# Decoder layer with routed experts: base rows gathered in the slot that uses them, two transpose groups placed side by side, and another order at the start of self-attention

## The reference

```python
x = x + attn(layernorm(x))               # attn(r) = r + p @ v, q = layernorm(r): 4 heads of 128,
                                         # 2048 fixed keys and values, p = relu(q @ k.T)**2
x = x + xattn(layernorm(x), ctx, mask)   # 16 heads of 64 over 128 context rows, softmax
x = x + ffn(layernorm(x))
# ffn: a shared SwiGLU (512 -> 1024 -> 512) and routed experts, top 1 of 32
e = argmax(x @ gate_w);  xs = x * sigmoid(max(x @ gate_w))
routed = (silu(xs @ Wg[e]) * (xs @ Wu[e])) @ Wd[e]     # Wg, Wu: 32 x 512 x 1024, Wd: 32 x 1024 x 512
out = shared(x) + routed
```

## Time and profile before

| | us |
|---|---|
| median of 3 runs (2825.84 to 2826.16) | 2826.04 |
| profiled execution | 2824.46 |
| its span, first to last instruction | 2822.8 |
| PE busy in it | 2761.5 (98%) |
| DVE busy | 1783.8 (63%) |
| POOL busy | 1063.0 (38%) |

### The profile page before, as it was taken

How to read it: one execution, slowest core, us unless ns; L and a number is a source line. 1 busy time by engine, 2 the same in 40 slices (tenths; PEclk the granted TensorE clock), 3 DMA queues, 4 the chain that set the end, 5 groups by cost and what they waited for, 6 DMA issues and landing times.

```text
span 2822.8 us, 46193 instructions
## 1 busy us (share of the span) xinstructions
PE 2761.5 (98%) x13287; PEld 2279.2 (81%) x13289; DVE 1783.8 (63%) x2600; ACT 1592.6 (56%) x2748; POOL 1063.0 (38%) x692
## 2 busy tenths in 40 slices
PE   7999999999999999999999999999999999999998
PEld 6888888888878888788778888887788888888886
DVE  6556565666876665667653333346795765677776
ACT  7888888888765554566621111112675644465665
POOL 6888888887622221122200000000342422333333
PEclk9999999999999999999999999999999999999999
DMA  1000000002231102110321111113896865787884
GB/s 64 27 27 11 26 26 26 11 30 63 83 98 46 45 30 90 39 37 27 112 93 63 60 59 59 59 59 111 323 355 211 326 217 166 257 299 239 294 288 174
DMA packets 191367, 326.90 MB, mean 116 GB/s; under 512 B 23592, under 2 KB 49192, under 8 KB 190784
## 3 DMA queue, kind: packets, MB, share of 16 engines
q1 hardware_dynamic: 180016, 300.81, 31.1%
q0 software_dynamic: 11280, 25.20, 2.6%
HBM read 288.95 MB, written 48.76 MB: 120 GB/s over the span
## 4 chain that ended last, share of the span: by engine, by line
PE 79%; issue 9%; DVE 5%; ACT 2%; POOL 2%; DMA 1%; ACTq 0%; DVEq 0%; POOLq 0%; SPq 0%
PE d_pG L1993 8%; PE d_pU L1993 8%; PE a_pS L47 4%; PE a_pS L49 4%; PE a_pS L48 4%; PE a_pO L47 4%; PE a_pO L49 4%; PE a_pO L48 4%; PE d_pD L49 3%; PE d_pD L47 3%; PE d_pD L48 3%; PE c_pD L49 2%; PE c_pD L47 2%; PE c_pG L47 2%; PE c_pD L48 2%
## 5 line engine op out<-in xcount | busy, mean ns | idle before, releaser
L158 POOL TENSOR_TENSOR a_pL<-a_p,a_pH 128x1024 fp32r<-128x1024 f32 x256 | 618.3, 2418 | 152.3 <-DVE a_p L345 149.9
L345 DVE TENSOR_TENSOR a_p<-a_r,a_pS 128x1024 f32<-128x1024 f32 x256 | 312.2, 1220 | 259.4 <-ACT a_r L166 254.2
L1229 DVE TENSOR_TENSOR e_wL<-e_raw,e_wH 128x1024 fp32r<-128x1024 f32 x384 | 450.1, 1217 | 33.8 <-PE d_pU L1993 23.1
L1224 ACT CAST e_wH<-e_raw 128x1024 fp32r<-128x1024 f32 x384 | 384.5, 1054 | 85.6 <-PE d_pD L49 59.5
L683 POOL TENSOR_TENSOR b_S<-b_S,b_ri 128x512 f32<-128x512 f32 x128 | 133.2, 1041 | 478.5 <-DVE b_ri L844 478.5
L166 ACT ACTIVATE a_r<-a_pS 128x1024 f32<-128x1024 f32 x256 | 261.8, 1023 | 78.8 <-PE a_pS L49 76.7
L166 ACT ACTIVATE a_pH<-a_r 128x1024 fp32r<-128x1024 f32 x256 | 271.9, 1062 | 9.1
L1473 POOL DMA_INDIRECT out<-d_og,c_iw x46 | 124.0, 2695 | 340.5 <-DVE d_og L1867 340.5
L700 ACT ACTIVATE b_S<-b_S,b_nm 128x128 f32<-128x128 f32 x512 | 198.9, 395 | 32.6 <-DVE b_nm L839 32.3
L47 PE MATMUL a_pS<-a_qH,a_kH 128*128 (+1 forms) x512 | 205.1, 401 | 2.3 <-DVE a_p L345 1.2
L47 PE MATMUL a_pO<-a_pH,a_vH 128*128 128x512 f32 x512 | 200.2, 391 | 1.5 <-POOL a_pL L158 1.5
(11 more groups left out here) (305 smaller groups left out, 7230.1 us busy)
## 6 DMA issues: line engine op xcount, KB each, us to landing
e_raw<-in_L_ffn_routed_gate_w SPq DMA_DIRECT2D x256, 256.0 KB, 4.6
e_raw<-in_L_ffn_routed_up_w SPq DMA_DIRECT2D x256, 256.0 KB, 5.7
e_raw<-in_L_ffn_routed_down_w SPq DMA_DIRECT2D x128, 512.0 KB, 6.6
a_xb<-in_x SPq DMA_DIRECT2D x8, 1024.0 KB, 5.5
x<-a_base SPq DMA_DIRECT2D x32, 256.0 KB, 2.3
b_xr<-x SPq DMA_DIRECT2D x32, 256.0 KB, 3.5
x<-b_xr SPq DMA_DIRECT2D x32, 256.0 KB, 3.0
c_xb<-x SPq DMA_DIRECT2D x32, 256.0 KB, 2.9
```

The lines of the kernel that those rows point to most:

```text
L158: nc.gpsimd.tensor_tensor(pL[:, j % RING, :, :], p[:, j % 2, :, :], pH[:, j % RING, :, :].bitcast(F32), ALU.subtract).then_inc(s["low"], 1)
L345: v.tensor_tensor(p[:, j % 2, :, :], r[:, j % 2, :, :], pS[j % 2][:, :, :], ALU.mult).then_inc(s["p"], 1)
L1224: copy(self.wH[n][:, :, :], self.raw[n][:, :, :]).then_inc(self.s["high"], 1)
L1229: unit.tensor_tensor(self.wL[n][:, :, :], self.raw[n][:, :, :], self.wH[n][:, :, :].bitcast(self.F32), self.sub).then_inc(self.s["low"], 1)
```

## The change

In the routed slots, POOL now gathers the base rows for slot t inside slot t, after the scatter of t-1 has landed and ahead of the scatter of t. One index tile, `c_ib`, serves both, so the copy into `c_iw` is gone, and so are the gathers of base rows ahead of the slots and behind the last one. PE runs `slot_x_transpose` directly behind `h_transpose(0)` and ahead of the last gate/up chunk. At the start of self-attention, ACT makes key piece 0, normalises head 0, makes piece 1 and `a_qH`, and only then pieces 2 and 3; DVE makes `a_kL` 0 and 1, the query head, and then `a_kL` 2 and 3; PE waits for the key pieces in pairs.

```diff
@@ self-attention, ACT
-        for n in range(KC):
+        def k_high(n):
             act.wait_ge(s["kvt"], n + 1)
             high(kH[:, n * KC:(n + 1) * KC, :], piece(k_ps[n])).then_inc(s["kvH"], 1)
+        k_high(0)
         act.wait_ge(s["own"], LINKS)
         for t in range(GT):
             normalize_first(t, slice(0, P), "first")
+        k_high(1)
         q_high(0, 0)
+        k_high(2)
+        k_high(3)
@@ self-attention, DVE
-        for n in range(KC):
+        for n in range(2):
             split_low(kL, kH, k_ps[n], n, n)
...
         q_low(0, 0)
+        for n in range(2, KC):
+            split_low(kL, kH, k_ps[n], n, n)
@@ self-attention, PE
-        pe.wait_ge(s["kvL"], KC)
...
+                if first and h == 0 and c < 2:
+                    pe.wait_ge(s["kvL"], 2 * c + 2)
@@ routed experts, POOL: ahead of the slots, in a slot, behind them
-        gather_base(0)
...
             pool.wait_ge(ds["turn"], 16 * t + 16)
-            nc.gpsimd.tensor_copy(iw[:, :], index[:, bass.ds(t, 1)]).then_inc(ds["iw"], 1)
+            gather_base(t)
             pool.wait_ge(ds["zero"], 2)
-            pool.wait_ge(ds["iw"], t + 2)
+            pool.wait_ge(ds["ib"], t + 2)
             pool.wait_ge(ds["sum"], t + 2)
-            indirect_dma(ds["turn"], out=out, out_offset=indirect(ap=iw[:, 0:1], axis=0), in_=og[:, :], in_offset=None)
-            pool.wait_ge(ds["b_in"], 16 * t + 16)
-            gather_base(t + 1)
+            indirect_dma(ds["turn"], out=out, out_offset=indirect(ap=ib[:, 0:1], axis=0), in_=og[:, :], in_offset=None)
...
-        pool.wait_ge(ds["b_in"], 16 * used + 16)
@@ routed experts, PE
             h_transpose(0)
+            slot_x_transpose(ds["x_in"], 16 * t + 16)
             gate_up(e, 1, (KC - 1,))
-            slot_x_transpose(ds["x_in"], 16 * t + 16)
```

More of the change, by code:

```diff
@@ L1270, in feed_forward @@
     starts, ends = c.at(c.end, "starts", [EXP, EXP], BF), c.at(c.end, "ends", [EXP, EXP], BF)
-    ix, iw = (c.at(c.end, n, [P, 1], I32) for n in ("ix", "iw"))
+    ix = c.at(c.end, "ix", [P, 1], I32)
     first_silu = c.at(c.end, "first", [1, 1], F32)
@@ L1328, in feed_forward @@
     ds = {n: ctx.enter_context(nc.semaphore("d_" + n)) for n in
-          "zero ix ib iw x_in b_in turn xt xH xL silu h ht hH hL used sum".split()}
+          "zero ix ib x_in b_in turn xt xH xL silu h ht hH hL used sum".split()}
     SL = 16
@@ L1465, in _ @@
         bound = pool.to_reg(TOK - 1)
-        nc.gpsimd.memset(iw[:, :], 0).then_inc(ds["iw"], 1)
+        nc.gpsimd.memset(ib[:, :], 0).then_inc(ds["ib"], 1)
         pool.wait_ge(s["logit"], GROUPS)
@@ L1486, in gather_base @@
             pool.wait_ge(ds["zero"], 2)
-            pool.wait_ge(ds["ib"], t + 1)
+            pool.wait_ge(ds["ib"], t + 2)
             indirect_dma(ds["b_in"], out=bg[:, :], out_offset=None, in_=base, in_offset=indirect(ap=ib[:, 0:1], axis=0))
-        pool.wait_ge(ds["iw"], 1)
+        pool.wait_ge(ds["ib"], 1)
         pool.wait_ge(rs["indexed"], 1)
```

## The result

The changed kernel took 2830.63 us (median of 22 runs, 2826.81 to 2838.99), the kernel before in the same session 2825.88 us (22 runs, 2824.89 to 2827.91): ratio 1.0018, 95% interval 1.0012 to 1.0023. So it is 4.75 us slower, against +3.4 forecast. The interval lies wholly above 1, so the slowdown is real; it is small enough to stay within the 0.2% that was set as the bound of "no change". What was not forecast is the spread: 12 us between its runs, 3 us between those of before.

A forecast was written before the change was run, and what follows sets the result against it. PE's own list and its waits were taken to bound the kernel. 5.9 - 0.8 - 2.0 + 0.3 = +3.4 us on 2826.04 gave 2829.4 us; range 2821.5 to 2848 us, the forecast's own 2826 to 2834.

The forecast's parts named there:

- The wait that decides: In the routed slots, `d_og` waits for the late base gather: 9 slots at 0.65 us, +5.9 us.
- Steps 1 to 5: Slot of 2083.42 us: scatter lands 2088.6, row gather over, copy ends 2089.4, gather in 2090.3, lands 2096.3; `d_og` 0.85 us late.
- tied slots: Routed slots that end with PE waiting for DVE's `d_h`, PE and DVE almost level: 20 of 46.
- step 3: POOL's copy into `c_ib` asks at 2088.7, gets in between two L1229 at 2089.2, ends about 2089.4.
- Rival 2: POOL's copy misses the gap (2848 us) or starves through DVE's train (2904 us); chance 0.22, the starving 0.04 of it.
- rival 1: The base gather lands in time for `d_og`, so the 5.9 us fall away: 2823.5 us; chance 0.2.
- The transposes: On PE, eight transposes side by side save 0.03 us in each of 26 slots that PE paces: -0.8 us (0 to -2.1).
- step 2: POOL's `gather_x`, its rows turned 1.44 us earlier, starts about 2085.6 instead of 2088.20 and is over by 2087.9.
- The tail: Behind the last `d_og`, POOL's copy, step and extra base gather go: -2.0 us (0 to -2.0).
- The start: In self-attention, two key pieces ahead of ACT's last normalising move the first relu from 20.09 to 20.4: +0.3 us (-0.5 to +0.5).
- 3 (a price for changing kind): PE pays for changing between transposes and matmuls; merging saves some 0.14 us in each of 26 slots: 2820.4 us; chance 0.1.

The follow-up runs named there:

- turn_only: The kernel before with only the transposes of the next slot's rows moved directly behind `h_transpose(0)`: 2824.38 us, ratio 0.9998.
- base_free: The changed kernel with the scatter's own index copy `c_iw` back and the base gather ahead of the wait for the scatter: 2821.61 us, ratio 0.9987.
- free_old_turn: base_free with the transposes in their old place, behind the last gate/up chunk: 2822.08 us, ratio 0.9990.
- base_only: The changed kernel without the moved transposes and without the new start of self-attention: 2838.11 us, ratio 1.0045.
- two_copies: The changed kernel with a second index copy between the wait for the landed scatter and the base copy `c_ib`: 2844.82 us, ratio 1.0068.
- look2: The changed kernel as it is, profiled once more: one run, 2831.05 us.

## Why the prediction was right

**The wait that decides (forecast +5.9 us, measured about +8).** Steps 1 to 5 stand in the rows of the slot of 2064.50 us: the scatter down 5.24 us after its issue ended where 4.9 was taken, copy 0.26 us in the gap, gather in at T + 6.65, `d_og` late 0.72. Where the gap was met the delay was 0.34 to 1.03 us in 15 tied slots of three profiles, mean 0.81 (0.65 taken). Where it was missed, it was 2.03 to 2.68 in three (2.5 taken). The margin of step 3 was as narrow as the prediction had it: in the three profiles the 24 base copies behind a fully held scatter that began by T + 5.64 met the gap, and the four that began from T + 5.74 to T + 5.88 missed it (slot 44, where the scatter was down early, is not counted). What was off is the count and the mixture. Nine tied slots were forecast, all meeting the gap; there were six, with none to two misses among them. Six, because after a gather that got in at T + 6.6 the next scatter was not held, so of neighbouring full slots only every other one is hit. The prediction took the 16 fully held scatters over unchanged; 11 were left, and the group fell from 124.0 to 100.5 us. The two errors, fewer slots and longer delays, partly cancel, which is luck: 6 x 0.81 = 4.9, and 1.0 to 1.4 for each miss. Rival 2 was thus no separate case but part of the likeliest one, with 0 to 2 misses instead of nine.

**A misread row.** The prediction says that `d_bg` was ordered a slot ahead, that the gather of 2085.33 serves the slot after, and that there were over 9 us to spare. Where the scatter was not held for the train it was so, with 6 to 12 us to spare (slot 37 aside). In the 16 slots behind a fully held scatter the kernel before, too, gathered the base rows in the slot that uses them, at T + 1.91: the gather of 2085.33 landed at 2091.3 and served the `d_og` of 2095.43, with 4.1 us to spare. The steps did not use the wrong figure. With the right one the price comes out in one line: the change moved this gather from T + 1.91 to T + 6.65, 4.7 us, and 4.1 were spare, which leaves 0.6 us late.

**The gathers' landing.** In the slot of 2064.50 us it took 2077.23 - 2071.15 = 6.1 us, as the earlier trace rows had it. The Trainium skill (DMA: Bandwidth & Descriptors, "Anatomy of one DMA") would give some 2.6 us as an estimate, by which rival 1 would have come true. No late slot here agrees (6.0 to 6.6 us).

**The transposes (forecast -0.8 us).** Measured -0.92 (turn_only) and -0.95 (base_free against free_old_turn). The change's PE in the slot of 2318.17 us, against the earlier trace rows:

```profile
2318.17 0.60 PE L2007 MATMUL d_pT<-ident,d_h 128*128 128x128 f32 x4
2318.61 0.60 PE L1986 MATMUL d_pX<-ident,d_xg 128*128 128x128 f32 x4
2318.96 0.48 PE L1996 MATMUL d_pG<-e_wH,d_xH 128*128 128x512 f32 x1
2319.28 0.40 PE L1996 MATMUL d_pU<-e_wH,d_xH 128*128 128x512 f32 x1
```

From the first transpose to the second matmul it is 1.11 us, less 0.23 for the matmul: 0.88 us for eight, twice the 0.44. By this view nothing is gained, and yet PE-paced slots of at most three pieces are 0.02 to 0.06 us shorter; where these hundredths lie stays open. What the prediction missed altogether is the indirect worth of the earlier turning, some 6 us, which only base_only shows: it counted on POOL's times with the new turning in step 2, but never priced the same edit without it.

**The tail (forecast -2.0 us).** Measured -2.4. POOL at the end has no gather behind the last scatter, against the earlier trace rows:

```profile
2808.95 0.19 POOL L1492 COPY c_ib<-c_index 128x1 int32 x1
2809.93 1.02 POOL L1480 DMA_INDIRECT d_bg<-base,c_ib  x1 [0.78 <-POOL c_ib L1492]
2818.52 1.02 POOL L1480 DMA_INDIRECT out<-d_og,c_ib  x1 [7.57 <-DVE d_og L1870]
```

**The start (forecast +0.3 us).** The first relu came at 20.47 us, forecast 20.4, by the ACT list as told. But 0.27 us of the 0.38 is a later first `a_kH` (10.87 against 10.60), which is no part of the change: the term measures +0.1 and was too large. With the 0.27 taken off, `a_qH` stood at 16.35 (forecast 16.45), and the relu 2.40 us behind the start of the last normalising (2.49 taken): these two tenths are what was mis-sized.

**What is left.** The terms as measured give some +8.3 - 0.9 - 2.4 + 0.1 = +5.1 us, the profiled span +4.1 and the median +4.75. The stretch ahead of the slots is 0.96 us shorter than before although its start is 0.38 later, and without it the profile would lie further from the forecast; that part is luck too. The windows of 1086 to 1089 us, before and then after, show one reason:

```profile
1086.00:1089.00 3.00, 3.00 (x11) 2.44 (x10) 2.89 (x4) 2.52 (x10) 0.93 (x1) 0.56 0.01 3
```

```profile
1086.00:1089.00 3.00, 2.63 (x13) 1.83 (x11) 3.00 (x5) 2.75 (x10) 0.72 (x1) 1.00 0.01 3
```

In the profile before the granted clock was 0.56 there, in the one after 1.00. Such stretches come and go between executions: one stands at 1084 to 1089 us in seven of the twelve profiles. The one that fell on slot 0 was worth 1.5 us, so two profiles can't settle a part of that size; a count of one kind of slot can.

Of the rivals, 1 (lands in time) and 3 (a price for changing kind) are refuted by the rows: `d_og` waited in every profile of the change, and no slot fell below 17.69 us.

## What to carry to other kernels

Saving one small buffer can tie a load to the landing of the store ahead of it; look where that chain ends against the moment the load is wanted, and put the load ahead of the wait in the queue, as base_free does, before pricing anything else. To price such a move, first measure how long before its use the load lands now, in each kind of slot: here 4.1 us in the slots that mattered. A step that must hit a gap of some tenths between two instructions of another engine has two prices, here 0.8 and 2.4 us, and the number of misses will differ between executions: forecast a mixture, and expect the spread to grow. Parts of a change that lie on one queue are to be priced alone as well as together; here one was worth 0.9 us by itself and 6 more beside the other.

## What the runs showed of the hardware

- A wait can cost more than its length: behind 1.99 us of idle time PE's granted clock was 0.64 for 4.33 us, some 1.5 us on top. In the twelve profiles PE stood for 1.9 us or more ahead of a slot nine times, and six times the clock was down behind it (1.94 to 2.71 us of idle time, two_copies and look2); in slots 1 to 44 it was down nowhere else. It is not the length alone: PE resumed at full clock after 2.41 and 2.06 us in the changed kernel's profile and after 1.97 us in two_copies.
- The scatter's hold of 4.6 us goes with the gather before it. In the changed kernel's profile 11 scatters took 4.6 us, all behind a base gather that got in at T + 4.3; the ten behind one that got in at T + 6.6 or T + 7.8, in the same kinds of slots and asking at the same place in DVE's train (T + 13.6 in slot 6), took 1.2 us. free_old_turn shows the same behind its row gather, which gets in as late, in 25 of 31 slots with nine or twelve pieces, not in all, and in look2 one of nine scatters behind a late gather took 2.3 us. The Trainium skill (SBUF — State Buffer, "Who interferes with whom") says that a DVE instruction with two SBUF inputs contends with a GpSimd instruction that reads SBUF for a shared read port, an exclusive lock. The copy agrees (1.16 and 1.19 us instead of 0.26 when it starts inside an L1236). It stays open why the scatter sometimes waits for the whole train and sometimes hardly at all. What sets it was not settled.
